# A transpose moved off TensorE: 32x32 turns on VectorE and a bounce through DRAM in 128 B pieces

## The reference, cut to what matters

```python
w1 = W1[language_ids]; w2 = W2[language_ids]
h = relu(einsum('bsh,bha->bsa', x, w1) + b1)            # 512 -> 128
x = x + layernorm(x + einsum('bsa,bah->bsh', h, w2) + b2) * gamma + beta      # "x1" below
h = gelu(einsum('bni,ih->bnh', x, W1) + b1)             # 512 -> 2048
x = x + concat(einsum(h, W2) + b2,                      # 2048 -> 384, shared
               einsum(h, We[expert]) + be)              # 2048 -> 128, by expert
```

## Time and profile before

| | |
|---|---|
| median of 3 runs | 1446.96 us (1446.64 to 1447.46) |
| span of the profiled execution, first to last instruction | 1444.7 us |
| TensorE busy | 1437.8 us, 6444 matmuls |
| VectorE busy | 959.4 us |
| ScalarE busy | 525.2 us |
| GpSimd busy | 679.3 us |
| DMA moved | 263.02 MB, 127908 packets |
| granted TensorE clock | 1.000 |

### The profile page before, as it was taken

One profiled execution on the slowest core, in us unless ns is written; L12 is line 12 of the kernel. 1 busy time (PEld: TensorE's weight loads), 2 busy tenths in 40 slices (PEclk: granted clock), 3 DMA queues, 4 the chain that ended last, 5 costly groups with the idle time before them and its releaser, 6 DMA issues.

```text
span 1444.7 us, 19133 instructions
## 1 busy us (share of the span) xinstructions
PE 1437.8 (100%) x6444; PEld 1186.4 (82%) x6444; DVE 959.4 (66%) x1589; ACT 525.2 (36%) x856; POOL 679.3 (47%) x644
## 2 busy tenths in 40 slices
PE   9999999999999999999999999999999999999999
PEld 6878888888888888888888888888888888888887
DVE  7999776785576755677556776568655686544434
ACT  5733453322533235232342323333244322432231
POOL 6987456451483513844148441474423844342101
PEclk9999999999999999999999999999999999999999
DMA  7857466554556445564464644646546454354332
GB/s 228 290 174 258 175 247 227 180 189 140 176 213 206 158 160 180 200 208 146 160 214 165 208 165 142 238 155 207 183 130 248 147 186 160 114 215 160 132 110 88
DMA packets 127908, 263.02 MB, mean 182 GB/s; under 512 B 12226, under 2 KB 84674, under 8 KB 119748
## 3 DMA queue, kind: packets, MB, share of 16 engines
q1 hardware_dynamic: 118020, 158.78, 34.5%
q10 hardware_dynamic: 9792, 103.03, 18.4%
HBM read 224.02 MB, written 37.75 MB: 181 GB/s over the span
## 4 chain that ended last, share of the span: by engine, by line
PE 94%; POOL 3%; DVE 2%; issue 1%; ACT 0%; POOLq 0%; DVEq 0%; ACTq 0%
PE down L259 16%; PE down L257 16%; PE down L258 16%; PE up_b L258 5%; PE up_b L259 5%; PE up_b L257 5%; PE up_c L257 4%; PE up_c L259 4%; PE up_c L258 4%; PE up_a L258 4%; PE up_a L257 4%; PE up_a L259 4%; PE aux L521 1%; PE aux L259 1%; PE aux L258 1%
## 5 line engine op out<-in xcount | busy, mean ns | idle before, releaser
L257 PE MATMUL down<-w,g 128*128 128x512 f32 x1024 | 400.9, 391 | 0.0
L259 PE MATMUL down<-w,g 128*128 128x512 f32 x1024 | 399.1, 390 | 0.0
L258 PE MATMUL down<-w,g 128*128 128x512 f32 x1024 | 398.9, 390 | 0.0
L1333 POOL TENSOR_TENSOR w<-w_raw,ones 128x256 fp32r<-128x256 f32 x125 | 92.9, 743 | 546.3 <-DMA w_raw<-m_we 546.2
L912 DVE TENSOR_TENSOR g<-g_raw,g 128x512 fp32r<-128x512 f32 x256 | 235.2, 939 | 86.0 <-ACT g L680 86.0
L259 PEld LDWEIGHTS down<-w,g 128*128 128x128 f32 x1024 | 192.3, 188 | 40.0
L258 PEld LDWEIGHTS down<-w,g 128*128 128x128 f32 x1024 | 192.4, 188 | 39.2
L257 PEld LDWEIGHTS down<-w,g 128*128 128x128 f32 x1024 | 192.4, 188 | 39.2
L672 ACT ACTIVATE g_raw<-up_a,m_b_sb 128x512 f32<-128x512 f32 x64 | 44.2, 690 | 412.7 <-PE up_a L259 388.0
L907 DVE TENSOR_TENSOR g_raw<-up_b,s 128x512 f32<-128x512 f32 x63 | 43.5, 691 | 220.5 <-PE up_b L259 176.9
L680 ACT CAST g<-g_raw 128x512 fp32r<-128x512 f32 x256 | 159.0, 621 | 8.1
(11 more groups left out here) (234 smaller groups left out, 2516.9 us busy)
## 6 DMA issues: line engine op xcount, KB each, us to landing
w<-w_kept ACTq DMA_DIRECT2D x55, 1792.0 KB, 7.7
w<-w_kept SPq DMA_DIRECT2D x56, 768.0 KB, 5.0
w_raw<-m_we SPq DMA_DIRECT2D x128, 128.0 KB, 4.6
out<-resid SPq DMA_DIRECT2D x64, 256.0 KB, 5.0
xTs_raw<-xT SPq DMA_DIRECT2D x56, 256.0 KB, 3.1
xs<-x SPq DMA_DIRECT2D x56, 256.0 KB, 5.9
w_kept<-w SPq DMA_DIRECT2D x8, 1792.0 KB, 8.4
aw_raw<-a_w SPq DMA_DIRECT2D x29, 256.0 KB, 4.8
```

The lines of the kernel that those rows point to most:

```text
L257: eng.matmul(bank, a_hi, b_hi, start=opens, stop=False, skip_group_check=True)
L258: eng.matmul(bank, a_hi, b_lo, start=False, stop=False, skip_group_check=True)
L259: return eng.matmul(bank, a_lo, b_hi, start=False, stop=closes, skip_group_check=True)
L1333: eng.tensor_tensor(hi, values, ones[:, :, :].to_broadcast([P, 2, PART]), ALU.mult).then_inc(pool_eh[b], 1)
```

## The change

`pe_transpose` is no longer called for pairs 1 to 7, and the waits that guarded its banks go with it. In its place:

- VectorE turns each finished tile of x1 (128 tokens by 512 features) in 32x32 blocks, one instruction for each tile, 8 for each pair (`dve_turns`). Batch 0's four tiles are turned at the end of step 4 and in step 5, batch 1's in steps 5 and 6. There is one buffer `turned` for both batches, in the place of xTs, so batch 1's first turn waits until all of batch 0's has been stored.
- SyncE stores each turned tile in 4 DMAs of 64 KB, one for each quarter of the partitions (`keep_turned`), 32 DMAs for each pair. A contiguous piece in DRAM is 32 tokens, 128 B, so a DMA has 32 x 16 = 512 pieces.
- SyncE loads the blocks back with features on the partitions, 8 DMAs of 256 KB for each pair (`load_blocks`), B12 in step 6, B11, B22 and B21 in step 7. It waits for the landing of all stores of the batch.
- ScalarE and VectorE read the blocks from SBUF instead of the banks (`act_block_hi`, `dve_b_lo`, `dve_t1` and so on); the copies of B12 go away.
- VectorE's order in steps 5 to 7 is rewritten: T1 and B11's low part stand ahead of `dve_down_sum` in step 7, the sum of c21 of step 5 moves between two moments, that of step 7 into step 7. SyncE's early loads for the pair after (`sp_early`) move from step 5 to the end of step 7, and in pair 0 `keep_w1` of step 5 stands behind the stores of batch 0, that of step 7 behind the loads of the blocks.

```diff
+    turned = sb("turned", [P, KC * Q, TT, B32], f32, "xTs")
+    x1_turned = nc.dram_tensor("x1_turned", [PAIRS, 2, KC, P, TOK], f32, kind="Internal").ap()
...
+    TURNED = {B11: (0, 0), B21: (0, 2), B12: (1, 0), B22: (1, 2)}
+    def block_landed(eng, m, of, c):
+        b, k = TURNED[of]
+        eng.wait_ge(in_turned[b][k + c], m.front(16, 16))
...
@@ pe_step
-        if k == 0:
-            eng.wait_ge(dve_c21, seven(i, 0))
-            pe_transpose(eng, i, 0, 2, up_b)
...
-            pe_transpose(eng, i, 0, 3)
-        if m and k == GROUPS - 1:
...
-            pe_transpose(eng, m, 1, 0, up_b)
-            pe_transpose(eng, m, 0, 0)
...
-            pe_transpose(eng, m, 0, 1)
...
-            pe_transpose(eng, m, 1, 1, up_a)
...
-            pe_transpose(eng, m, 1, 2, up_c)
...
-            pe_transpose(eng, m, 1, 3)
...
+    def act_block_hi(eng, m, of, c):
+        block_landed(eng, m, of, c)
+        eng.copy(bo[:, of, c, HI, :], block_raw(of, c)).then_inc(act_bhi, 1)
...
+    def dve_turn(eng, m, b, t):
+        n = b * TT + t + 1
+        eng.wait_ge(dve_x1, m.count(2 * TT, n))
+        if b == 0 and t == 0:
+            eng.wait_ge(pe_a1, m.count(2 * KC, 2 * KC))
+        if b == 1 and t == 0:
+            eng.wait_ge(kept_turned[0], m.front(16 * Q * TT, 16 * Q * TT))
+        eng.transpose(turned[:, :, t, :], x1[:, b, t, :].rearrange("p (j r) -> p j r", r=B32)).then_inc(dve_turned, 1)
...
+    def dve_t1(eng, m, c):
+        block_landed(eng, m, B12, c)
+        block_landed(eng, m, B11, c)
...
@@ dve_step
+        if m and k == 5:
+            dve_turns(eng, m, 0, 2)
+        if m and k == GROUPS - 1:
+            dve_t1(eng, m, 0)
+            dve_b_lo(eng, m, B11, 0)
         if k % 2 == 0:
             if k >= 2:
                 dve_down_sum(eng, i, 0, k - 1)
...
+        if m and k in (5, 6):
+            dve_turns(eng, m, 1, 2 * (k - 5))
...
+            if k == 5:
+                dve_sum_c21(eng, i, k)
             dve_moments(eng, m, b, t + 1)
+        if m and k == 4:
+            dve_turns(eng, m, 0, 0)
...
+    def keep_turned(eng, m, b):
+        blocks = x1_turned[m.index, b, :, :, :].rearrange("c (j i) (t q e) -> q i (c j) t e", j=Q, q=Q, t=TT)
+        for t in range(TT):
+            eng.wait_ge(dve_turned, m.front(2 * TT, b * TT + t + 1))
+            for q in range(Q):
+                eng.dma_start(blocks[q, :, :, t, :], turned[q * B32:(q + 1) * B32, :, t, :]).then_inc(kept_turned[b], 16)
+
+    def load_blocks(eng, m, of):
+        b, k = TURNED[of]
+        eng.wait_ge(kept_turned[b], m.front(16 * Q * TT, 16 * Q * TT))
+        if of == B12:
+            eng.wait_ge(dve_t, m.count(8, 0))
+        else:
+            eng.wait_ge(pe_p[{B11: 1, B21: 2, B22: 3}[of]], seven(m, 0))
+        for c in range(2):
+            eng.dma_start(block_raw(of, c), x1_turned[m.index, b, k + c, :, :]).then_inc(in_turned[b][k + c], 16)
...
@@ sp_pair
+            if m and k == GROUPS - 1:
+                load_blocks(eng, m, B11)
+            if m and k == 5 and i is not first:
+                keep_turned(eng, m, 0)
...
+                    if k == 5:
+                        first_w2(eng, k, experts)
+                        keep_turned(eng, m, 0)
...
-                    keep_w1(eng, k)
+                    if k < GROUPS - 1:
+                        keep_w1(eng, k)
...
+            if m and k == 6 and i is not first:
+                keep_turned(eng, m, 1)
+                load_blocks(eng, m, B12)
             if k % 2 == 0 and (i is not first or k > 0):
...
                 load_experts(eng, k, experts)
...
+            if m and k == GROUPS - 1:
+                load_blocks(eng, m, B22)
+                load_blocks(eng, m, B21)
```

More of the change, by code:

```diff
@@ L139, in build @@
     out_done = [sems(f"out_done{b}_", TT) for b in range(2)]
+    dve_turned, kept_turned = sem("dve_turned"), sems("kept_turned", 2)
+    in_turned = [sems(f"in_turned{b}_", KC) for b in range(2)]
     pe_p = [None, *sems("pe_p", 8)[1:]]
@@ L816, in act_step @@
             return
-        if k == 0 and i is not pairs[1]:
-            act_b22_hi(eng, i, 1)
         if k > 0:
@@ L865, in act_step @@
         act_g(eng, i, k, C22)
-        if i is first and k == GROUPS - 1:
-            act_t_hi(eng, m, T1, 1)
-            act_t_hi(eng, m, T3, 0)
-            act_t_hi(eng, m, T2, 0)
-            act_b22_hi(eng, m, 1)
         if i is first and k in (3, 5):
             act_w2_hi(eng, k)
-        if m and k == GROUPS - 1 and i is not first:
+        if m and k == GROUPS - 1:
+            if i is first:
+                act_t_hi(eng, m, T1, 1)
+            act_block_hi(eng, m, B22, 0)
+            act_block_hi(eng, m, B22, 1)
             act_t_hi(eng, m, T3, 0)
@@ L1135, in dve_first_step @@
             dve_w2_lo(eng, k - 1)
-        if k == GROUPS - 1:
-            dve_b_lo(eng, m, B11, 0)
-            dve_t1(eng, m, 0)
         if k % 2 == 0:
@@ L1185, in dve_step @@
         if k > 0:
-            dve_sum_c21(eng, i, k - 1)
+            if not (m and k == 6):
+                dve_sum_c21(eng, i, k - 1)
             dve_g_lo(eng, i, k - 1, C21)
         else:
-            if before(i) is not first:
-                dve_sum_c21(eng, before(i), GROUPS - 1)
-                dve_t3_t2(eng, i, 1)
-                dve_b_lo(eng, i, B22, 1)
             dve_g_lo(eng, before(i), GROUPS - 1, C21)
@@ L1257, in dve_step @@
             dve_g_lo(eng, i, k, C22)
+        if m and k == GROUPS - 1:
+            dve_t3_t2(eng, m, 0)
+            dve_b_lo(eng, m, B22, 0)
+            dve_sum_c21(eng, i, k)
+            dve_t3_t2(eng, m, 1)
+            dve_b_lo(eng, m, B22, 1)
     def pool_aw_lo(eng, m, b, n):
@@ L1460, in pool_step @@
             pool_expert(eng, i, 1, k)
+            if m:
+                for of, c in t_order(m)[2:4]:
+                    pool_t_lo(eng, m, of, c)
     def load_xT(eng, m, b, k):
@@ L1467, in load_xT @@
             eng.wait_ge(pe_a1, m.count(2 * KC, b * KC + k // 2 * 2))
+            if b == 0 and k < 2 and m is not pairs[1]:
+                eng.wait_ge(kept_turned[1], m.front(16 * Q * TT, 0))
         eng.dma_start(xT_tile(m, b, k)[1][:, LO, :], xT[m.batch(b), k, :, :]).then_inc(in_xT[b][k], 16)
@@ L1645, in sp_pair @@
                     load_x(eng, m, 1, (2, 3))
-            if after and k == 5:
-                sp_early(eng, after, next_language)
             if i is not first and k == 0:
@@ L1669, in sp_pair @@
                 load_experts(eng, k, experts)
+            if i is first and k == 6:
+                keep_turned(eng, m, 1)
+                load_blocks(eng, m, B12)
+            if m and k == GROUPS - 1:
+                load_blocks(eng, m, B22)
+                load_blocks(eng, m, B21)
+            if i is first and k == GROUPS - 1:
+                keep_w1(eng, k)
+            if after and k == GROUPS - 1:
+                sp_early(eng, after, next_language)
         if i is first:
```

159 lines of the change are left out of this document (73 added, 86 removed).

## The result

The changed kernel takes 1464.28 us (1459.93 to 1470.95, 4 runs) where the kernel before, on the same chip, takes 1447.21 us (1446.64 to 1448.60): a ratio of 1.012, 95% interval 1.0092 to 1.0149. It is slower by 17 us, and the forecast was 16 us faster. The profiled execution is the slowest of the four, with a span of 1469.1 us against 1444.7 us before, so what follows explains 24.4 us of span, and says at the end what differs from run to run.

What follows compares the result with a forecast made beforehand. TensorE was taken as the bound, busy 1437.8 of 1444.7 us. 1444.7 - 24.6 + 7 x 1.1 + 1 = 1428.8, plus 2.3 for the median, gave 1431 us; range 1421 to 1490, forecast case 1426 to 1438.

Steps and rivals of the forecast that it cites:

- Wait A: Step 5, batch 1's first turn waits for batch 0's stores, c22's sum behind it: 0 at 13 ns a piece.
- wait B: Step 7, T1 waits for B11's landing ahead of the down sums, so p7 waits for u2: 1.1 us each pair.
- pair 0: Raw load in the first pair, behind batch 0's stores, is 8.6 us late: 1 us lost, up to 4.
- The sum: Profiled span 1444.7 less the transposes' gain plus the waits: 1428.8 us; median of the runs 2.3 us higher.
- The removal: TensorE's transposes leave pairs 1 to 7: 56 calls at 0.44 us, 24.6 us gained.
- The turn: VectorE's new 128x512 instruction, 56 in all: 0.68 us each, at most twice that, costing nothing by itself.
- The piece: Time a DMA engine takes to store 128 B: 13 ns taken, 27 ns as upper bound.
- the dear-piece rival: Stores at 27 ns a piece: 4.6 and 3.8 us of waits in steps 5 and 7 each pair, 1482 us; chance 0.22.
- The rule that the prediction quotes: DMA stores: line rate from 512 B up, read-modify-write below; quoted as an argument against the change.
- a second pass: Read-and-write rival: each stored piece takes two passes, 54 ns, 29 us each pair, about 1626 us; chance 0.11, or worse.

Runs made afterwards that it cites:

- m1_ports: Separate measurement, none of the kernel's work: VectorE subtractions with two SBUF inputs or one in PSUM, with and without GpSimd; two SBUF inputs 685 ns alone, 1568 beside GpSimd.
- e9_light: Changed kernel, but in pairs 1 to 7 ScalarE writes a second rounded copy instead of GpSimd making the T blocks' low parts (work left out); 1437.01 us.
- e13_bank: Changed kernel, plus ScalarE copying each half block of pairs 1 to 7 into one PSUM bank, from which VectorE reads it; 1442.82 us.
- e2_raw_first: Changed kernel, with pair 0's raw load of w1 for the next pair issued ahead of batch 1's stores; 1462.01 us.
- e10_pair0: e2_raw_first, plus in pair 0's last step ScalarE's g and weight work ahead of B11 and VectorE's weight low parts before T1; 1460.38 us.
- e12_order2: e11_order, but in pair 0 the second layer's last weights are taken later and GpSimd makes its new weights' low part before T1's; 1445.76 us.
- e17_bank_part: e14_bank_order, but ScalarE copies only B11 and B22 into the bank; B21 is read from SBUF; 1429.53 us.
- e11_order: Changed kernel with e10_pair0's orders, g's low part of C21 earlier, and VectorE's T1, down sums, u2 and q sums reordered in steps 7 and 0; 1452.62 us.
- e14_bank_order: e12_order2 with e13_bank's edit, so mended orders and blocks read from PSUM; 1438.44 us.
- e6_2kb: Changed kernel storing the same bytes with as many DMAs in 2 KB pieces, so the blocks that come back hold other data; 1460.14 us.

## Why the prediction was wrong

**The step that failed** is the costing of the change's waits as only A, B and pair 0. VectorE's T and low parts of the blocks keep their number and, but for T1 and B11's low part, their place in steps 7 and 0, so their change of source was put at nothing, without a reason. But their source moved from a PSUM bank into SBUF, and there they run beside GpSimd at up to 1.78 us instead of 0.68. That makes the low part of g of C21 late (wait C), 2.1 to 2.5 us in each of six pairs and 5.3 us in one: with the 0.5 us inside pair 0, 19.6 us. Shown by m1_ports (1568 against 685 ns), by e9_light (18 us of it gone with GpSimd's work) and by e13_bank (16.6 us gone with the source back in PSUM). The Trainium skill, "SBUF — State Buffer", section "SBUF: two separate sides", says that a VectorE instruction with two SBUF inputs and a GpSimd instruction that reads SBUF exclude each other for a whole instruction. The runs agree: 1.57 and 1.70 us side by side, 0.68 and 1.27 with one input in PSUM. I hadn't weighed that against the edit, and the rows I had quoted already carried a sign of the price: in the earlier trace rows line 912, two SBUF inputs, takes 2.27 us for two instructions, while lines 892 and 902, with a PSUM input, take 0.69 each.

**Pair 0** was put at 1 us, up to 4. It was 8.0 us, and for another reason than the raw load: late blocks (landed at 191) and late second-layer weights (195) hold ScalarE and VectorE with ready work behind them. e2_raw_first and e10_pair0 show that neither cure helps by itself; e12_order2, with two orders changed at once, leaves 2.8 us of it.

**The clock** wasn't foreseen. Some 15 us of the span went to TensorE at 1.2 GHz around the waits, 11.7 of them while it had work. So a wait can cost more than its length: behind the wait of 2.47 us at 745 the next seven matmuls took 3.09 us (747.61 to 750.70) instead of 1.59.

**The sum** of the span, by these terms: the forecast said 1428.8. Add wait C 19.6, pair 0's 8.0 - 1.0, the clock's 11.7, and take off 0.5 for wait B (7.7 forecast; 7.2 measured, in the waits for u2 beyond those of before): 1466.6, against the 1469.1 measured. Most of the 2.5 us left is in how a wait is counted. A matmul's record is 0.39 us long and the next can start 0.23 us after it, so a listed wait is 0.16 us short: from 744.75 to 747.61 TensorE lost 2.63 us, and 2.47 are listed. The changed kernel has 13 listed waits more than the kernel before, which makes 2.1 us. For e17_bank_part, 1444.7 - 24.6 + 4.2 us of listed waits beyond those of before = 1424.3, against 1426.8, again 2.5 us short; its clock falls only after the last matmul. For e9_light and e13_bank the same sum with the clock's 2.5 and 3.4 us is 1.8 and 2.5 us short, for e11_order, e12_order2 and e14_bank_order 7 to 9 us. By the starts of the matmuls, these three have many delays of less than 0.3 us in pairs 1 to 7 that the list doesn't name, 5 to 6 us in all, beside the 0.16 us for each listed wait.

**What was right.** The removal: no transposition is left on TensorE after pair 0, and the sums above hold with 24.6 us. The turn: 0.68 us taken, 0.672 in m1_ports. The piece: 13 ns taken, 12.1 measured, so the dear-piece rival fell with its mechanism, though its side of the result came true; that 1464 us lies in its bracket is chance. The rule that the prediction quotes from the Trainium skill, "DMA: Bandwidth & Descriptors", Specifications, agrees as far as the line rate goes (128 B in 12.1 ns are 10.6 B in a nanosecond, 512 B in 27 ns are 19.0); a second pass, which the prediction made of it at 54 ns, doesn't show in the time of a piece. Wait A: VectorE does stand before the turn of batch 1,

```profile
694.71 1.30 DVE L997 STREAM_TRANSPOSE turned<-x 128x512 f32<-128x512 f32 x2 [3.88 <-DMA x_turned<-turned]
```

but c22's sum, next at 695.94, is in time: TensorE never waits for it. Wait B: the sum came out, but by luck. There is no 1.1 us in each pair: of the three waits one, of 0.7 us, was there before the change, and one is 5.5 us. In the profiles of e2_raw_first and e10_pair0, which keep the turns, the stores and (but in pair 0) T1's place, the same line has 0.7 and 1.3 us in all. The row behind the wait of 5.5 us (VectorE, step 7):

```profile
910.79 0.88 DVE L1013 TENSOR_TENSOR t<-b,bo_raw 128x512 f32<-128x512 f32 x1 [7.54 <-issue]
```

The runs of the changed kernel lie 11 us apart, those of e13_bank, with T1 in the same place, 18 us, those of e12_order2 and of the kernel before 2 us. VectorE's waits before T1 come to 14.1 us in the changed kernel's profile, which is of its slowest run, to 4.6 us in that of e2_raw_first and to 2.3 us in that of e6_2kb. That B11's landing, late in more or fewer pairs, makes the spread is argued from these, not shown.

## What to carry to other kernels

When an operand moves from PSUM to SBUF, or back, price every reader again, even if no instruction is added: look at what GpSimd does at the same time. Where an engine's list has an instruction with a late transfer in front of ready work, fix the list until no late transfer is in front; each cure showed the next one (e2, e10, e12). And count a new wait of TensorE with the half clock behind it.

## What the runs showed of the hardware

- VectorE, 128x512 f32, two SBUF inputs: 685 ns alone, 1568 ns beside a GpSimd instruction with two SBUF inputs, which itself takes 1702 ns. With one input in PSUM: 682 ns beside GpSimd, and GpSimd 1270 ns. A turn of 128x512: 672 ns beside GpSimd. (GpSimd's 1039 ns beside the turns is another instruction, the sum of a tile with itself, and can't be set against the 1270.)
- A store in pieces of 128 B takes a DMA engine 12.1 ns for each piece, and the same bytes in 2 KB pieces made no measurable difference to the kernel's time (1460.14 against 1464.28 us, ratios with overlapping intervals).
- Some waits of TensorE of 2.1 us and more, not all, were followed by a stretch at a granted clock of 0.50, down to 10 matmuls in 4 us instead of 19. The length of the wait doesn't decide it: with waits for g of 2.07 and 2.26 us the clock fell, with others of 2.40 and 2.46 us it did not. In the kernel before, whose longest wait after the start is 0.7 us, there was no such stretch.
